# One 8 MB load of the first MLP weights, split into three loads that are issued as their target regions come free

## The reference, cut to what matters

```
xn   = layernorm(x)
g    = xn @ gate_w + gate_b                  # 1024 -> 2048, two halves, silu each
u    = (xn * gate) @ state_w + state_b
Bm   = gate_gate @ state_w + state_b
y    = scan(exp(-delta), delta * Bm * u)     # h = dA * h + dBu over the tokens
x    = x + y @ out_w + out_b
x2   = layernorm(x)
x    = x + gelu(x2 @ mlp_w1 + mlp_b1) @ mlp_w2 + mlp_b2      # 1024 -> 4096 -> 1024
x    = x + (silu(z @ wg.T) * (z @ wu.T)) @ wd.T              # z = layernorm(x), 1024 -> 3072 -> 1024
```

## Time and profile before

| | us |
|---|---|
| runs shown, two | 7143.14 and 8051.44, median 7597.29 |
| profiled execution | 7146.75 |
| span of its slowest core (core 7) | 7144.9 |
| spans of the 8 cores | 7102.7 to 7144.9 |
| PE busy (matmul), share of the span | 5601.7, 78% |
| DVE busy | 2132.2, 30% |
| ACT busy | 1455.2, 20% |

### The profile page before, as it was taken

One profiled execution on the slowest core, in us unless ns is written; L12 is line 12 of the kernel. 1 busy time (PEld: TensorE's weight loads), 2 busy tenths in 40 slices (PEclk: granted clock), 3 DMA queues, 4 the chain that ended last, 5 costly groups with the idle time before them and its releaser, 6 DMA issues.

```text
span 7144.9 us, 71046 instructions; the slowest of 8 cores (7102.7 to 7144.9 us)
## 1 busy us (share of the span) xinstructions
PE 5601.7 (78%) x25792; PEld 2660.4 (37%) x25792; DVE 2132.2 (30%) x3789; ACT 1455.2 (20%) x2024; POOL 13.1 (0%) x28
## 2 busy tenths in 40 slices
PE   0559788697886977878878788778887698786979
PEld 0224333243333433334433344333443244333434
DVE  1240333303333134321344123350233503324032
ACT  0122112221122111221112211222112121122211
POOL 0000000000000000000000000000000000000000
PEclk8779898798987999889988899889998799898999
DMA  9971342123411234012440224302242113321134
GB/s 136 132 133 54 109 139 77 71 71 101 152 60 65 83 112 159 36 78 70 129 149 24 100 68 131 125 24 106 89 144 98 67 51 115 125 90 71 66 103 150
DMA packets 160070, 690.50 MB, mean 97 GB/s; under 512 B 18866, under 2 KB 18995, under 8 KB 133684
## 3 DMA queue, kind: packets, MB, share of 16 engines
q1 hardware_dynamic: 155956, 608.37, 25.6%
q0 software_dynamic: 3776, 77.60, 6.5%
HBM read 696.38 MB, written 77.59 MB: 108 GB/s over the span
## 4 chain that ended last, share of the span: by engine, by line
PE 71%; DVE 12%; DMA 7%; issue 5%; ACT 3%; another core or an unknown queue 1%; DVEq 0%; SPq 0%; ACTq 0%; POOL 0%; POOLq 0%
PE pb L346 28%; PE pb L927 12%; PE pb L1100 9%; PE pb L1112 9%; PE pb L1195 7%; DMA REG<-s_mlp 3%; PE pb L399 2%; PE pb L426 2%; DMA REG<-s_fd 1%; DMA TTR<-x_in 1%; ACT TTR L1032 1%; DVE REG L745 1%; PE pb L682 1%; DVE X L791 1%
## 5 line engine op out<-in xcount | busy, mean ns | idle before, releaser
L346 PE MATMUL pb<-FMB,REG 128*128 128x512 bf16 x4096 | 903.7, 384 | 308.1 <-DMA REG<-s_mlp 306.9
L927 PE MATMUL pb<-M1R,TTR 128*128 128x512 bf16 x4096 | 887.2, 379 | 9.7 <-ACT M1R L363 8.8
L346 PE MATMUL pb<-REG,M1R 128*128 128x512 bf16 x3072 | 712.4, 397 | 176.8 <-DVE REG L751 123.1
L399 PE MATMUL pb<-IDF,TTR 128*128 128x128 f32 x1536 | 296.5, 345 | 565.8 <-ACT TTR L1032 275.7
L1100 PE MATMUL pb<-FMB,REG 128*128 128x512 bf16 x3072 | 725.7, 379 | 7.9 <-DVE FMB L1048 7.9
L1112 PE MATMUL pb<-FMB,REG 128*128 128x512 bf16 x3072 | 725.7, 379 | 0.1
L346 PEld LDWEIGHTS pb<-FMB,REG 128*128 128x128 bf16 x4096 | 403.6, 99 | 804.8 <-issue 335.1
L1195 PE MATMUL pb<-M1R,REG 128*128 128x512 bf16 x3072 | 672.9, 380 | 27.3 <-DMA REG<-s_fd 23.1
L943 DVE TENSOR_SCALAR TTR<-pb,CB_M 128x512 f32<-128x512 f32 x128 | 96.1, 751 | 1972.1 <-PE pb L927 1972.1
L1144 DVE TENSOR_SCALAR REG<-pb 128x512 f32<-128x512 f32 x384 | 265.6, 692 | 1084.4 <-PE pb L1112 1084.4
L927 PEld LDWEIGHTS pb<-M1R,TTR 128*128 128x128 bf16 x4096 | 400.1, 98 | 494.0 <-issue 15.3
(11 more groups left out here) (98 smaller groups left out, 3145.9 us busy)
## 6 DMA issues: line engine op xcount, KB each, us to landing
TTR<-s_mlp SPq DMA_DIRECT2D x128, 1024.0 KB, 4.8
REG<-s_fg SPq DMA_DIRECT2D x384, 256.0 KB, 2.7
REG<-s_fu SPq DMA_DIRECT2D x384, 256.0 KB, 2.7
REG<-s_fd SPq DMA_DIRECT2D x128, 768.0 KB, 4.6
TTR<-x_in SPq DMA_DIRECT2D x16, 2048.0 KB, 9.6
M1R<-s_gate SPq DMA_DIRECT2D x8, 4096.0 KB, 13.2
y_out<-X POOLq DMA_DIRECT2D x16, 2048.0 KB, 7.1
s_mlp<-w_mlp POOLq DMA_DIRECT2D x2, 8192.0 KB, 87.0
```

Source lines behind the costliest of these rows:

```text
L346: ins = t.matmul(psum[bank][:, 0:512], wsb[:, w_tile(m, k) * P:(w_tile(m, k) + 1) * P], rhs_fn(s, k), start=(k == 0), stop=(k == n_k - 1))
L399: ins = t.transpose(psum[bank][:, tau * P:(tau + 1) * P], src[:, tau * 1024 + c * P: tau * 1024 + (c + 1) * P], IDF[:])
L927: ins = t.matmul(psum[bank][:, 0:512], A_RING[:, slot + k * P:slot + (k + 1) * P], M1[:, k * 512:(k + 1) * 512], start=(k == 0), stop=(k = ...
```

## The change

The load in `fwm1` is removed, and with it its waits for DVE, ACT and PE. In its place there are three `load_w`, each at the place of the program from which its region is free:

- `mlp1a`: 2 MB for m = 8 to 15, right behind the load of the out-projection weights, after the last matmul of Bm
- `mlp1b`: 4 MB for m = 16 to 31, after the last instruction of the scan on DVE
- `mlp1c`: 2 MB for m = 0 to 7, after the last matmul of the out-projection of s = 1

`mm_stage` gets an argument `m_order` and takes a function for `w_ready`; PE then waits for the load of a tile before that tile's matmuls. `m1_0` and `m1_1` go through the tiles in the order 8 to 31, then 0 to 7. The number of matmuls and of bytes stays.

```
+            load_w(f"mlp1a{b}", W_BIG[:, 16384:24576],
+                   s_mlp1[:, 8:16].rearrange("p m k f -> p (m k f)"),
+                   CM["cast_mlp1"], state_last_mm)
...
+            scan_done_dve = pr.mark("dve")
+            load_w(f"mlp1b{b}", W_BIG[:, 24576:40960],
+                   s_mlp1[:, 16:32].rearrange("p m k f -> p (m k f)"),
+                   CM["cast_mlp1"], scan_done_dve)
...
             ssm1 = emit_out_mm(1, [ssmT0_done])
+            outmm1_pe = pr.mark("pe")
+            load_w(f"mlp1c{b}", W_BIG[:, 8192:16384],
+                   s_mlp1[:, 0:8].rearrange("p m k f -> p (m k f)"),
+                   CM["cast_mlp1"], outmm1_pe)
+            def mlp1_ready(m, b=b):
...
+            mlp1_m_order = list(range(8, 32)) + list(range(0, 8))
...
-            mlp1_region_waits = [pr.mark("dve"), pr.mark("act"), ssmT1_done]
-            def fwm1(sy):
...
-            sync_sec(fwm1)
...
-                CM[f"mlp1_{b}"], func=AF.Gelu,
+                mlp1_ready, func=AF.Gelu,
...
-                subs=(0,))
+                subs=(0,), m_order=mlp1_m_order)
```

More of the change, by code:

```diff
@@ L324, in mm_stage @@
                      extra_pe_waits=(), banks=(0, 1, 2, 3), subs=(0, 1),
-                     group_waits=None):
+                     group_waits=None, m_order=None):
             sem = eng
@@ L328, in mm_stage @@
             nbk = len(banks)
-            idx = [(s, m) for s in subs for m in range(n_m)]
+            idx = [(s, m) for s in subs
+                   for m in (m_order if m_order is not None else range(n_m))]
             fills = []
             def fpe(t):
-                pr.wait(t, "pe", w_ready)
+                if not callable(w_ready):
+                    pr.wait(t, "pe", w_ready)
                 for mk in extra_pe_waits:
@@ L336, in fpe @@
                 for i, (s, m) in enumerate(idx):
+                    if callable(w_ready):
+                        pr.wait(t, "pe", w_ready(m))
                     if group_waits is not None:
@@ L858, in build_program @@
             ssm1 = emit_out_mm(1, [ssmT0_done])
+            outmm1_pe = pr.mark("pe")
[3 more added lines that the diff above has]
+            def mlp1_ready(m, b=b):
+                if m < 8:
+                    return CM[f"mlp1c{b}"]
+                if m < 16:
+                    return CM[f"mlp1a{b}"]
+                return CM[f"mlp1b{b}"]
+            mlp1_m_order = list(range(8, 32)) + list(range(0, 8))
             fills_t20 = tm_to_fm_pe(T2, [CM[f"t2{b}_0"]], "act")
@@ L979, in build_program @@
                 extra_pe_waits=list(x2n_by_sub[1]) + [mlp2_0_pe],
-                subs=(1,))
+                subs=(1,), m_order=mlp1_m_order)
             emit_mlp2(1, ssmT1_done, m1_1)
```

## The result

| | before | changed |
|---|---|---|
| median of all runs | 7563.63 us (10 runs) | 7214.76 us (11 runs) |
| lowest run | 7143.14 us | 6838.46 us |
| ratio of the comparison | | 0.9586, 95% interval 0.9561 to 0.961 |

The changed kernel is faster by 4.1%. The forecast was 6834 us, 0.9562 of the profiled execution of before, in a range of 6795 to 6925. The lowest run is 4.5 us from the forecast; the median, 7214.76 us, lies 290 us above the range, so as a statement on that median the prediction was wrong. In more than half of the runs of either kernel, the first profiled execution of the changed one (7258.9 us) among them, the cores of one or both dies have a lower granted clock and take several per cent longer: the medians contain these runs, the ratio leaves them out.

What follows compares the result with a forecast made beforehand. TensorE was taken to set the time, so its idle time lengthens the span. From 7146.75 us, -306.9 (idle time), +1.6 (waits and seam) and -7.5 (clock) gave 6833.9 us, range 6795 to 6925.

Steps and rivals of the forecast that it cites:

- The idle time (-306.9 us): PE's eight waits for mlp_w1 ahead of the first MLP product, one per block, vanish entirely: -306.9 us.
- division of a wait: PE's 36.57 us idle before one block's MLP product: 14.3 us waiting for DVE's norm, 22.2 us the load itself.
- The seam: Between last transposes and MLP product, with PE's three waits instead of one: 0.2 us each block, +1.6 us.
- The clock (-7.5 us): MLP product of s = 0 starts less slowly without idle time: 9.6 of 17.1 us slow start remain, gaining 7.5.
- The moved loads (0, and +20 us in the first block): Earlier loads disturb neither scan, matmuls nor out-projection: 0; first block's out-projection weights perhaps 20 us later, kept for the range.
- the bound for the second piece: In the first block, mlp1b lands by 471 us even with slow loads, against a product starting at 472.7.
- A wait in the middle of the product: Sign that the prediction is wrong: PE waits inside the MLP product, at tiles 16 or 0.
- The sum: Whole kernel: 7146.75 - 306.9 + 1.6 - 7.5 = 6833.9 us, against the profiled execution of before.
- A wait remains: Rival: MLP product still starts only after DVE's norm of s = 1, giving back 114 us: 6948 us; chance 0.04.
- Nothing is gained: Rival: the time saved before the MLP product is handed on to a later wait: 7147 us; chance 0.01.
- The loads collide: Rival: out-projection late by 20 us in the first block, a few us in others: 6882 us; chance 0.08.
- Slower: the clock gives way: Rival: eight cores running dense lose the full clock in dense stages: 7742 us; chance 0.03.

Runs made afterwards that it cites:

- the changed kernel, third time: The changed kernel itself, unedited, run again as reference in the last comparison: ratio to before 0.9553; profiled execution 6826.26 us.
- the early single load: Against the changed kernel, mlp_w1 comes in one 8 MB load, issued at the end of the out-projection of s = 1: ratio to before 0.9663.
- the two with 22 us left: Against the changed kernel: all three loads at the old place (7014.9 us, 0.983); only the third piece there, tiles 0 to 31 (0.9816).
- the two repetitions: The changed kernel itself, unedited, run again beside other variants as their reference: ratios to before 0.9593 and 0.9553.
- the third piece late, tiles in the order of the changed kernel: Against the changed kernel, only the third piece is issued at the old place behind DVE's norm, tiles 8 to 31 then 0 to 7: ratio to before 0.957.
- the casts held: Against the changed kernel, the last three casts start only once the first block's out-projection weights have landed: ratio to before 0.959.

## Why the prediction was right or wrong

**The idle time (-306.9 us): right.** The group of the MLP's first products had 308.1 us of idle time ahead of it, of which 306.9 were the load. In the changed kernel, third time, it has 1.2 (groups of PE by line and shape: busy us, mean ns, idle before; the first row is of before):

```profile
L346 PE MATMUL pb<-FMB,REG 128*128 128x512 bf16 x4096 | 903.7, 384 | 308.1 <-DMA REG<-s_mlp 306.9
...
L350 PE MATMUL pb<-FMB,REG 128*128 128x512 bf16 x4096 | 896.1, 382 | 1.2
```

My division of a wait into 14.3 us for DVE and 22.2 us of transfer was tested by the early single load (4.28 us left in the fourth block) and by the two with 22 us left. The seam, for which I took 1.6 us, is at most these 1.2.

**The clock (-7.5 us): right in sum, by luck, not in kind.** I took 1.2 us of slow start for each block. The first seven products of s = 0 of the changed kernel, third time, sum to 395.77 us, 7.9 above 7 x 55.41: 1.13 each. But they are of two kinds, as the products of the second and fifth block show (PE's timeline of the changed kernel, third time):

```profile
1290.65 55.42 PE L350 MATMUL pb<-FMB,REG 128*128 128x512 bf16 x256
...
3769.22 57.03 PE L350 MATMUL pb<-FMB,REG 128*128 128x512 bf16 x256
```

Two of the seven start at the full clock and lose nothing, five lose 1.3 to 1.7 us, where all eight lost 1.8 to 2.7 before. That their mean is the 1.2 us of the out-projection is chance. The windows say the same (columns as in the earlier trace rows). The fourth block's product of this profile runs its first 4 us at 1.00, the level of 2.4 GHz; the low stretch fell into the transposes ahead of it, where 2930 to 2934 us has 0.65:

```profile
2942.70:2946.70 4.00, 4.00 (x21) 1.86 (x20) 3.90 (x7) 2.01 (x3) 0.00 (x0) 1.00 0.67 227
```

On core 2 of the first profiled execution of the changed kernel these 4 us have 0.64, a mean over both levels, and the product takes 56.58 us. What decides which kind a block is, no run here shows.

```profile
2959.00:2963.00 4.00, 3.93 (x12) 1.55 (x12) 3.90 (x8) 0.80 (x1) 0.00 (x0) 0.64 0.75 266
```

**The moved loads (0, and +20 us in the first block): right in blocks 2 to 8, wrong in the first.** In blocks 2 to 8 nothing waits. In the first block I left open whether `mlp1a` shares the way with the out-projection's load or queues behind it. It queues behind: without it the out-projection starts no earlier, and with the first piece in front some 33 us later. This is also what the Trainium skill says (DMA: Bandwidth & Descriptors, Queues, rings and completion order); the runs agree. What I had wrong is the bound for the second piece, landed by 471 us even with all loads slowed by the casts. In the first block of the changed kernel, third time, two cores wait ahead of the 65th matmul, which is tile 16, for 1.8 and 3.4 us; this is core 3, on PE's timeline:

```profile
464.38 13.98 PE L350 MATMUL pb<-FMB,REG 128*128 128x512 bf16 x64
480.13 41.60 PE L350 MATMUL pb<-FMB,REG 128*128 128x512 bf16 x192 [1.77 <-DMA REG<-s_mlp]
```

So the piece was there at 480, not by 471. A wait in the middle of the product is one of the signs for which I had called the prediction wrong: the sign is there, in one block, at a price of 4.6 us at most in the profiles read. For the third piece I had given no bound beside the casts; without the order of tiles it costs up to 24.2 us.

**The sum: right in ratio, at its edge.** 0.9562 was forecast and 0.9586 measured, with 0.9561 as the lower end of the interval; the two repetitions gave 0.9593 and 0.9553. On 7146.75 us that is 6851 us, 17 us more than forecast. The third time, with 0.9553, it is 7 us less than forecast. None of the changed kernel's runs behind the 0.9586 has a profile, so what the 17 us are stays open. The first block is not it: its out-projection starts at 402 to 412 us before and at 396 to 406 in the changed kernel, third time. A candidate is a short spell of lower clock, as core 7, the slowest, has it in the profile of "the third piece late, tiles in the order of the changed kernel" (6851.58 us). One product takes 12 us more than its 55.41 there, in a stretch (546 to 704 us) with a granted clock of 0.82 (PE's timeline):

```profile
602.50 67.38 PE L350 MATMUL pb<-FMB,REG 128*128 128x512 bf16 x256
```

The changed kernel, third time, has no such spell on its slowest core.

**The number for the median: wrong.** The step that failed is the one in which I set the sum against the profiled execution alone and said of the median, 6% higher, "I don't forecast from it". The ratio of the sum, 0.9562, on the median of the two runs then shown would have been 7265 us, 50 us from the 7215 measured; the two medians themselves stand at 0.954. In the prediction's terms, the base of the sum was wrong (7146.75 us, where the kernel before has a median of 7563.63), and a time some 900 us higher was a rival of chance 0.03, one that the change would have to bring about, although one of the two runs of before had it already. The range, 6795 to 6925, was built from the ends of the terms and a few tenths of a per cent between executions, where the two runs shown were 908 us apart. The change did not cause this spread and did not remove it.

**The rivals.** "A wait remains" falls: the product runs beside DVE's norm. "Nothing is gained" falls. "The loads collide" exists in the first block alone and is small as long as the out-projection's load is first. "Slower: the clock gives way" falls as an effect of the change: the runs of before spread as far, and there are executions of the changed kernel, as the third time, whose slowest core has 1.00 in the dense stretches.

But I was wrong to say that the trace disagrees with the rule of the Trainium skill (TensorE: Matmul & The Clock Gate, Seeing it yourself), 13/16 of the clock once three cores of a die run dense matmuls. The first profiled execution of the changed kernel has just this level (13/16 is 0.8125) on cores 4 to 7, one die, but at different parts of their spans. Core 7 has it at the beginning and not at the end:

```profile
1475.00:1540.00 65.00, 65.00 (x249) 26.97 (x248) 10.72 (x31) 22.56 (x32) 0.00 (x0) 0.81 0.08 31
...
5976.00:6030.00 54.00, 54.00 (x252) 24.50 (x251) 0.42 (x1) 22.23 (x32) 0.00 (x0) 1.00 0.00 1
```

Core 4 has it the other way round:

```profile
1475.00:1540.00 65.00, 63.65 (x292) 28.82 (x296) 3.75 (x5) 10.46 (x16) 0.00 (x0) 1.00 0.23 80
5976.00:6030.00 54.00, 53.55 (x202) 22.41 (x206) 17.83 (x26) 7.76 (x13) 0.00 (x0) 0.81 0.43 125
```

Cores 6 and 7 are low from about 200 to 3440 us, cores 4 and 5 from about 4150 us to their end: spells of nearly the same length, at the start of one pair and at the end of the other. That is how it would look if the two pairs started milliseconds apart and the clock fell only while both ran. Each core's times count from its own start, so this is an argument and not shown; but dense stretches at 1.00 in a program of eight cores don't show that three cores of a die ran at the same time, and so they can't speak against the rule. Whether it holds here stays open.

## What to carry to other kernels

A load that waits for "everything so far" on several engines can be moved by asking, region by region, which instruction is the last to use it; here that was worth 240 of 307 us even without splitting. Where a load can't be early, split it and let the consumer begin with the piece that lands first, since only that piece's landing is waited for. And what runs once beside the first iteration (here casts of weights) needs its own look: it turned covers that were ample in seven blocks into waits in the first, and moving it wholesale only moved the wait.

## What the runs showed of the hardware that I had not expected

Loads issued by SP one behind the other are served in this order: in steady state three loads of 2, 4 and 2 MB release PE after 22 us (14.3 of them the wait for DVE) and cost no second wait. Beside the casts, putting one 2 MB load in front of another delays it by some 33 us (starts of the out-projection at 436 against 402 us on average), putting it behind by nothing (401 to 411 us without it, 396 to 406 with it).

The casts in flight cost the first block about the same on every core, but not on the same load. In the kernel before, PE waits on core 7 for 33.9 us for the state weights and for 19.8 us ahead of the out-projection, on core 3 for 2.7 and 47.2 us; less the scan's 17.3 us that is 32 to 37 us on the eight cores before and 30 to 35 in the changed kernel, third time. With the casts held, none of it is left. The casts cost their share wherever they stand, but where PE asks for nothing for 50 us most of it isn't seen.
